# Scores on four 32-row tiles with a bank each, and the products with the values in two blocks per group

## The chip, the cores and the metric

One NeuronCore of a Trainium2 chip runs the whole kernel. The metric is the device time of one execution in microseconds, lower is better. Engines: TensorE (PE in the profile, PEld for its weight loads), VectorE (DVE), ScalarE (ACT), GpSimd (POOL), SyncE (SP).

## The reference

A Flamingo-like layer: gated cross attention with 16 heads of 16, then a gated mixture of 8 experts with the two best per token. B = 32 batches, S = 56 query rows, T = 1500 context rows, D = 256. Only the attention is touched:

```python
q = proj(layernorm(x), Wq, bq)              # (B, 16, 56, 16)
k = proj(ctx, Wk, bk)                       # (B, 16, 1500, 16)
v = proj(ctx, Wv, bv)
scores = einsum('bhsd,bhtd->bhst', q, k) / 4
scores = clip(where(attend, scores, -10000), -50, 50)
probs = softmax(scores)
ctx = einsum('bhst,bhtd->bhsd', probs, v)
delta = layernorm(clip(rs, 0, 0.3) * (ctx @ Wo.T + bo)) * gamma + beta
x = x + tanh(g_xattn) * delta
x = x + tanh(g_ffn) * experts(layernorm(x))
```

## The kernel before, in words

The work goes by pairs of batches, 16 pairs. A batch's 1500 context rows are three groups of 500 (GC = 4 chunks of TC = 125 rows each), so a pair has six groups, q = 0 to 5, and 24 chunks. A step u on ScalarE and VectorE is two chunks, half a group. Everything is unrolled, each engine has one list of instructions in a fixed order, and semaphores alone tie the lists together.

All fp32 products of keys, values and scores are made of three terms in fp32r, high by high, high by low, low by high. `kv_part` (L578) makes keys and values of the group after the current one. It has four calls per group: half 0 or 1 (which 128 key columns, which two value chunks), part 0 or 1 (which 64 rows of the contraction). Keys run on one 64-row half of the array and values on the other at the same time; k_ps has a bank for each half, v_ps is one bank.

`scores` (L613) makes one chunk: positions in the partitions, heads by queries in the columns. The head dimension is 16, so four heads (64 rows) are taken in one product: the keys of 125 positions are the weights, and q_hi / q_lo, where each head's queries stand in columns of their own with zeros elsewhere (`q_diagonal`, L1110, with hmask), stream as 4 x 56 = 224 columns. Two such 64-row tiles run at a time, r = 0 and 1, each into its own bank; the two column blocks m share the bank. Chunks of even and odd number use two banks each out of the four of sc_ps, so that `scores` of one chunk can run while ScalarE reads the other (`wait(pe, exp_done, n - 1)`, L621).

`exps` (L892) is ScalarE's exponential of one chunk into prob, `clip` (L1273) VectorE's clamp, and `pv` (L631) the product of the probabilities with the values: 16 heads on four 32-column tiles with plain fp32, summed over a batch in o_ps. The keys leave k_ps in two steps: `k_hi_evac` (L878, the instruction is L883) on ScalarE and then `k_lo_evac` (L1057, L1060) on VectorE, which needs the first. `v_evac_step` (L1069, L1075) on VectorE empties v_ps.

TensorE's order in a group (`pair`, L711) is: PV of the four chunks of the group before, side work of `beside_pv`, part (0,0) of the next group's keys and values, scores of chunk c, part (0,1), scores of c + 1 and c + 2, part (1,0), scores of c + 3, part (1,1). Side work is there at q = 3 (ranks and router, query projection, output projection) and q = 5 (two transposes). Its results share a bank with the keys' second half, so it waits for `k_lo`. The first scores of a group wait for that group's low keys (L620).

Of the kernel before, what the change touches and what calls it, by code (L numbers as in the profile page):

```python
# [31 lines left out]
HW = HS * HD  # L32
NE = 8
# [21 lines left out]
CST = (P, NE, HS, KD, KD, PW, NE, NE * NE, CAP // SL, NU, 1, 2 * NS)  # L55
# [9 lines left out]
def gated_cross_attention_moe(nc, a, slot_rows, expert_rows, sums_dram, inv_dram, out):  # L65
# [5 lines left out]
    with ExitStack() as ctx:  # L71
# [121 lines left out]
        q_hi = sb("q_hi", [P, 2, KD, HS, S], fp32r, scope=att)  # L193
        q_lo = sb("q_lo", [P, 2, KD, HS, S], fp32r, scope=att)
# [346 lines left out]
        def _(pe):  # L541
# [71 lines left out]
            def scores(i, c):  # L613

                n = i * PC + c
                b, g = c // NC, c // GC
                if c % NC == 0:
                    pe.wait_ge(q_ready, 4 * i + 2 * b + 2)
                if c % GC == 0:
                    pe.wait_ge(k_lo, KD * (i * PG + g + 1))  # L620
                wait(pe, exp_done, n - 1)  # L621
                cs = slice(c % GC * TC, (c % GC + 1) * TC)
                for m in range(KD):
                    for term, (k, q) in enumerate(((kh, q_hi), (kh, q_lo), (kl, q_hi))):
                        for r in range(2):
                            rows = slice(r * HW, (r + 1) * HW)
                            last = pe.matmul(sc_ps[0:TC, 2 * (c % 2) + r, m * HS * S:(m + 1) * HS * S],  # L627
                                             k[rows, g % 2, m, cs], q[rows, b, m, :, :], start=term == 0, stop=term == 2)
                last.then_inc(scores_done, 1)

            def pv(i, c):  # L631
# [7 lines left out]
                for h in range(NH):  # L639
                    col, q = divmod(h, ST)  # L640
                    at = (h // HS % 2 * KD + h // (2 * HS)) * HS + h % HS
# [69 lines left out]
            def pair(i):  # L711
# [13 lines left out]
                for q in range(PG):  # L725
# [3 lines left out]
                    if first and q == 1:  # L729
                        pe.wait_ge(o_clear, 1)  # L730
                    if not (first and q == 0):
                        for d in range(GC, 0, -1):
                            pv(*((i, c - d) if q > 0 else (i - 1, PC - d)))
                    beside_pv(i, q, first, late, final)
                    if more:
                        kv_part(n, 0, slot, 0)
                    scores(i, c)
                    if more:
                        kv_part(n, 0, slot, 1)
                    if first and q == 0:  # L740
                        pe.wait_ge(v_evac, 2)
                    scores(i, c + 1)
                    if not more:
                        turn(0)
                    scores(i, c + 2)
                    if more:
                        kv_part(n, 1, slot, 0, freed.get(q, ()))
                    scores(i, c + 3)
                    if more:
                        kv_part(n, 1, slot, 1)  # L750
                    if q == PG - 2:
                        whole_lines(i)
# [124 lines left out]
        def _(act):  # L877
# [14 lines left out]
            def exps(i, c):  # L892

                n = i * PC + c
                act.wait_ge(scores_done, n + 1)
                wait(act, pv_done, n - PB + 1)
                act.activation(prob[0:TC, c % PB, :].rearrange("p (c n) -> p c n", c=2),  # L897
                               sc_ps[0:TC, 2 * (c % 2):2 * (c % 2) + 2, 0:NH * S // 2], ACT.Exp,
# [41 lines left out]
            def pair(i, first=False, late=False, final=False):  # L940
                for u in range(UN):
# [20 lines left out]
                    if half == 1:  # L962
                        exps(i, 2 * u + 1)
                    if not (final and q == PG - 1):
                        k_hi_evac(i * PG + q + 1, half, (q + 1) % 2)
                    if half == 0:
                        exps(i, 2 * u + 1)
# [64 lines left out]
        def _(dve):  # L1032
# [77 lines left out]
            def q_diagonal(dst, b, part):  # L1110
                shape = [P, KD, HS, S]
# [167 lines left out]
            def pair(i, first=False, late=False, final=False):  # L1279
                for u in range(UN):  # L1280
# [5 lines left out]
                    if u == 10 and not first:  # L1286
                        y_low(i - 1)
                    if half == 0:
                        if more:
                            v_evac_step(i * PG + q + 1, half, (q + 1) % 2)  # L1290
                        clip(i, 2 * u)
# [277 lines left out]
```

## Time and profile before

| | us |
|---|---|
| median of 3 runs | 1195.04 |
| lowest, highest | 1194.09, 1195.85 |
| profiled execution | 1202.38 |
| its span, first to last instruction | 1200.3 |
| TensorE's mean granted clock over the span, share of full | 0.981 |
| busy: TensorE products, loads | 1130.6, 1082.1 |
| busy: VectorE, ScalarE, GpSimd | 862.1, 664.2, 156.8 |

Products on TensorE are pipelined: a product's duration includes its way through the array, so the pace is read from the distance of starts, not from the durations. The attention stage fills the time up to about 1080 us, the experts the rest.

### The profile page before, as it was taken

How to read it: one execution, taken by the hardware profiler on the slowest of the kernel's cores; microseconds unless marked ns; L12 is line 12 of the kernel's file. 1: busy time of each engine (PE TensorE's matmuls, PEld its weight loads, DVE VectorE, ACT ScalarE, POOL GpSimd, SP SyncE). 2: the span in 40 equal slices, each digit the busy share in tenths (PEclk: the TensorE clock that was granted, in tenths of full speed). 3: DMA queues.
4: the chain of work that ended last, by engine and by line, in shares of the span. 5: the costliest groups of instructions: out<-in, count | busy, mean ns of one | idle time of the engine just before them, and what ended most of it. 6: DMA issues, size and time to landing. Idle time of an engine off the chain costs nothing.

```text
span 1200.3 us, 56000 instructions
## 1 busy us (share of the span) xinstructions
PE 1130.6 (94%) x24824; PEld 1082.1 (90%) x24824; DVE 862.1 (72%) x2003; ACT 664.2 (55%) x846; POOL 156.8 (13%) x186
## 2 busy tenths in 40 slices
PE   4799999999999999999999999999999999969884
PEld 4799999999999999999999999999999999968874
DVE  4467776777777776777777777777777777757677
ACT  1466565655556565656565556656565656534432
POOL 0000100010010101010111101010101101023431
PEclk9799999999999999999999999999999999989998
DMA  4223132222323233323222232323321222124306
GB/s 153 74 74 91 57 93 79 85 76 77 91 88 91 67 87 93 80 63 94 83 86 68 89 91 88 87 71 87 93 78 50 79 61 71 30 54 120 90 25 169
DMA packets 59487, 98.57 MB, mean 82 GB/s; under 512 B 14514, under 2 KB 42034, under 8 KB 59250
## 3 DMA queue, kind: packets, MB, share of 16 engines
q1 hardware_dynamic: 49538, 79.55, 23.9%
q10 hardware_dynamic: 6832, 8.92, 2.1%
q0 software_dynamic: 2880, 6.53, 1.5%
q8 instruction: 199, 3.26, 1.1%
q14 instruction: 38, 0.31, 0.1%
HBM read 70.32 MB, written 24.71 MB: 79 GB/s over the span
## 4 chain that ended last, share of the span: by engine, by line
PE 86%; issue 5%; DVE 5%; DMA 2%; POOL 1%; ACT 1%; SPq 0%; DVEq 0%; POOLq 0%; ACTq 0%
PE v_ps L601 22%; PE k_ps L604 21%; PE sc_ps L627 20%; PE o_ps L642 13%; PE k_ps L659 1%; PE sc_ps L544 1%; PE sc_ps L545 1%; PE k_ps L666 1%; PE sc_ps L546 1%; PE v_ps L692 1%; DVE acc L1509 1%; DVE h_sq L1438 1%; DVE acc L1452 1%; POOL rstd L460 0%; PE k_ps L805 0%
## 5 line engine op out<-in xcount | busy, mean ns | idle before, releaser
L897 ACT ACTIVATE prob<-sc_ps,m_bias 125x896 f32<-125x896 f32 x384 | 377.9, 1009 | 329.7 <-PE sc_ps L627 329.3
L601 PE MATMUL v_ps<-wv_hi,c_hi 64*125 64x256 f32 x1520 | 312.0, 285 | 2.7 <-DVE c_lo L1066 2.6
L604 PE MATMUL k_ps<-c_hi,wk_hi 64*128 64x500 f32 x760 | 306.8, 404 | 0.0
L601 PE MATMUL v_ps<-wv_lo,c_hi 64*125 64x256 f32 x1520 | 302.1, 279 | 0.0
L601 PE MATMUL v_ps<-wv_hi,c_lo 64*125 64x256 f32 x1520 | 301.9, 278 | 0.0
L604 PE MATMUL k_ps<-c_lo,wk_hi 64*128 64x500 f32 x760 | 294.0, 387 | 0.0
L604 PE MATMUL k_ps<-c_hi,wk_lo 64*128 64x500 f32 x760 | 293.2, 386 | 0.0
L1075 DVE TENSOR_TENSOR vst<-v_ps,rowv 125x512 f32<-125x512 f32 x191 | 131.3, 687 | 184.9 <-PE v_ps L601 184.9
L1277 DVE TENSOR_SCALAR prob<-prob 125x896 f32<-125x896 f32 x384 | 235.5, 626 | 21.3 <-ACT prob L897 21.1
L601 PEld LDWEIGHTS v_ps<-wv_hi,c_hi 64*125 64x125 f32 x1520 | 227.0, 185 | 16.6 <-issue 5.7
L627 PE MATMUL sc_ps<-q_hi,kh 64*125 64x224 f32 x1536 | 231.1, 268 | 7.1 <-ACT prob L897 7.1
L627 PE MATMUL sc_ps<-q_hi,kl 64*125 64x224 f32 x1536 | 232.5, 270 | 0.6 <-issue 0.6
L627 PE MATMUL sc_ps<-q_lo,kh 64*125 64x224 f32 x1536 | 232.7, 271 | 0.0
L601 PEld LDWEIGHTS v_ps<-wv_hi,c_lo 64*125 64x125 f32 x1520 | 230.4, 184 | 0.0
L601 PEld LDWEIGHTS v_ps<-wv_lo,c_hi 64*125 64x125 f32 x1520 | 229.3, 183 | 0.0
L627 PEld LDWEIGHTS sc_ps<-q_hi,kh 64*125 64x125 f32 x1536 | 198.7, 186 | 7.8 <-ACT prob L897 7.3
L642 PE MATMUL o_ps<-prob,vst 125*17 125x56 f32 x12288 | 179.9, 214 | 13.1 <-issue 8.5
L642 PEld LDWEIGHTS o_ps<-prob,vst 125*17 125x17 f32 x12288 | 158.7, 98 | 33.9 <-issue 25.6
L627 PEld LDWEIGHTS sc_ps<-q_hi,kl 64*125 64x125 f32 x1536 | 169.9, 187 | 1.0 <-issue 0.7
L627 PEld LDWEIGHTS sc_ps<-q_lo,kh 64*125 64x125 f32 x1536 | 168.4, 186 | 0.0
L883 ACT ACTIVATE kh<-k_ps,cst 128x500 fp32r<-128x500 f32 x192 | 130.3, 679 | 66.7 <-PE k_ps L604 66.7
L604 PEld LDWEIGHTS k_ps<-c_lo,wk_hi 64*128 64x128 f32 x760 | 142.3, 187 | 0.0
(193 smaller groups left out, 1664.3 us busy)
## 6 DMA issues: line engine op xcount, KB each, us to landing
raw<-in_ctxT SPq DMA_DIRECT2D x96, 500.0 KB, 3.8
slot_rows<-zero_row SPq DMA_DIRECT2D x112, 132.0 KB, 3.7
rows<-slot_rows SPq DMA_DIRECT2D x32, 132.0 KB, 2.1
w_raw<-in_we ACTq DMA_DIRECT2D x16, 256.0 KB, 5.1
rec<-inv_scratch SPq DMA_DIRECT2D x64, 56.0 KB
expert_out<-expert_rows SPq DMA_DIRECT2D x6, 448.0 KB, 7.3
xq<-in_x ACTq DMA_DIRECT2D x16, 112.0 KB, 4.0
xr<-in_x ACTq DMA_DIRECT2D x16, 112.0 KB, 3.7
```

The costliest lines, as they stand in the source:

```text
L544: pe.matmul(ps, w_h, m_h, start=first, stop=False)
L545: pe.matmul(ps, w_h, m_l, start=False, stop=False)
L546: return pe.matmul(ps, w_l, m_h, start=False, stop=last)
L601: v_last = pe.matmul(v_ps[0:TC, j * D:(j + 1) * D], c_s[v_rows, cs], w_m[v_rows, k, :], start=begin and j == 0, stop=end, skip_group_check ...
L604: k_last = pe.matmul(k_ps[:, half, 0:TG], w[k_rows, k, ws], c_m[k_rows, :], start=begin, stop=end)
L627: last = pe.matmul(sc_ps[0:TC, 2 * (c % 2) + r, m * HS * S:(m + 1) * HS * S], k[rows, g % 2, m, cs], q[rows, b, m, :, :], start=term == 0, ...
L642: last = pe.matmul(o_ps[q * 32:q * 32 + VW, col * S:(col + 1) * S], vst[0:TC, c // GC % 2, c % GC, h, :], prob[0:TC, c % PB, at * S:(at + ...
L659: last = pe.matmul(bank[:, m * PW:(m + 1) * PW], wq[:, k, m * P:(m + 1) * P], xnT[:, k, :], start=(k == 0), stop=(k == KD - 1))
L883: act.activation(kh[:, s, m, :], k_ps[:, m, 0:TG], ACT.Identity, bias=bk[:, m:m + 1]).then_inc(k_hi, 1)
L897: act.activation(prob[0:TC, c % PB, :].rearrange("p (c n) -> p c n", c=2), sc_ps[0:TC, 2 * (c % 2):2 * (c % 2) + 2, 0:NH * S // 2], ACT.Ex ...
L1075: dve.tensor_tensor(vst[0:TC, s, 2 * half:2 * half + 2, :, 0:HD], v_bank[0:TC, :].rearrange("p (j h d) -> p j h d", j=2, h=NH), bv[0:TC, : ...
L1277: dve.tensor_scalar(p, p, EXP_LO, EXP_HI, ALU.max, ALU.min).then_inc(clip_done, 1)
```

## The change

A product of the scores takes two heads, 32 rows, and 2 x 56 = 112 columns. Four tiles of 32 rows run side by side, each into a bank of its own. Two chunks are made in one call, and a bank holds both chunks' two column blocks; so a call of `scores` waits for all exponentials before it. Products and loads per chunk double from 12 to 24. `exps` reads one half of each of the four banks, 896 elements as before. In `pair` the order is: side work, scores of c and c + 1, parts (0,0) and (0,1), scores of c + 2 and c + 3, PV of c and c + 1, part (1,0), part (1,1), PV of c + 2 and c + 3. ScalarE takes both exponentials of a step ahead of the high keys. VectorE empties the value bank between the two clips in the first half, and after them in the second.

```diff
+QH = 2
+QW = QH * HD
-        q_hi = sb("q_hi", [P, 2, KD, HS, S], fp32r, scope=att)
-        q_lo = sb("q_lo", [P, 2, KD, HS, S], fp32r, scope=att)
+        q_hi = sb("q_hi", [P, 2, KD, QH, S], fp32r, scope=att)
+        q_lo = sb("q_lo", [P, 2, KD, QH, S], fp32r, scope=att)
...
-            def scores(i, c):
+            def scores(i, c0):
...
-                wait(pe, exp_done, n - 1)
-                cs = slice(c % GC * TC, (c % GC + 1) * TC)
-                for m in range(KD):
-                    for term, (k, q) in enumerate(((kh, q_hi), (kh, q_lo), (kl, q_hi))):
-                        for r in range(2):
-                            rows = slice(r * HW, (r + 1) * HW)
-                            last = pe.matmul(sc_ps[0:TC, 2 * (c % 2) + r, m * HS * S:(m + 1) * HS * S],
-                                             k[rows, g % 2, m, cs], q[rows, b, m, :, :], start=term == 0, stop=term == 2)
-                last.then_inc(scores_done, 1)
+                wait(pe, exp_done, n)
+                for c in (c0, c0 + 1):
+                    cs = slice(c % GC * TC, (c % GC + 1) * TC)
+                    for m in range(KD):
+                        at = (c % 2 * KD + m) * QH * S
+                        for term, (k, q) in enumerate(((kh, q_hi), (kh, q_lo), (kl, q_hi))):
+                            for r in range(ST):
+                                rows = slice(r * QW, (r + 1) * QW)
+                                last = pe.matmul(sc_ps[0:TC, r, at:at + QH * S], k[rows, g % 2, m, cs], q[rows, b, m, :, :],
+                                                 start=term == 0, stop=term == 2, tile_position=(r * QW, 0))
+                last.then_inc(scores_done, 2)
...
-                    at = (h // HS % 2 * KD + h // (2 * HS)) * HS + h % HS
+                    at = (h % (NH // KD) // QH * KD + h // (NH // KD)) * QH + h % QH
...
-                    if first and q == 1:
-                        pe.wait_ge(o_clear, 1)
-                    if not (first and q == 0):
-                        for d in range(GC, 0, -1):
-                            pv(*((i, c - d) if q > 0 else (i - 1, PC - d)))
                     beside_pv(i, q, first, late, final)
+                    if first and q == 0:
+                        pe.wait_ge(v_evac, 2)
+                    scores(i, c)
                     if more:
                         kv_part(n, 0, slot, 0)
-                    scores(i, c)
-                    if more:
                         kv_part(n, 0, slot, 1)
-                    if first and q == 0:
-                        pe.wait_ge(v_evac, 2)
-                    scores(i, c + 1)
-                    if not more:
+                    else:
                         turn(0)
                     scores(i, c + 2)
                     if more:
+                        if first and q == 0:
+                            pe.wait_ge(o_clear, 1)
+                        for d in range(2):
+                            pv(i, c + d)
                         kv_part(n, 1, slot, 0, freed.get(q, ()))
-                    scores(i, c + 3)
-                    if more:
                         kv_part(n, 1, slot, 1)
+                        for d in range(2, GC):
+                            pv(i, c + d)
...
-                act.wait_ge(scores_done, n + 1)
+                act.wait_ge(scores_done, n + 2 - c % 2)
                 wait(act, pv_done, n - PB + 1)
-                act.activation(prob[0:TC, c % PB, :].rearrange("p (c n) -> p c n", c=2),
-                               sc_ps[0:TC, 2 * (c % 2):2 * (c % 2) + 2, 0:NH * S // 2], ACT.Exp,
+                at = c % 2 * KD * QH * S
+                act.activation(prob[0:TC, c % PB, :].rearrange("p (r n) -> p r n", r=ST),
+                               sc_ps[0:TC, :, at:at + KD * QH * S], ACT.Exp,
...
                     exps(i, 2 * u)
-                    if half == 1:
-                        exps(i, 2 * u + 1)
+                    exps(i, 2 * u + 1)
                     if not (final and q == PG - 1):
                         k_hi_evac(i * PG + q + 1, half, (q + 1) % 2)
-                    if half == 0:
-                        exps(i, 2 * u + 1)
...
+                    clip(i, 2 * u)
+                    if half == 1:
+                        clip(i, 2 * u + 1)
+                    if more:
+                        v_evac_step(i * PG + q + 1, half, (q + 1) % 2)
                     if half == 0:
-                        if more:
-                            v_evac_step(i * PG + q + 1, half, (q + 1) % 2)
-                        clip(i, 2 * u)
-                        if more:
-                            k_lo_evac(i * PG + q + 1, half, (q + 1) % 2)
                         clip(i, 2 * u + 1)
-                    else:
-                        clip(i, 2 * u)
-                        clip(i, 2 * u + 1)
-                        if more:
-                            v_evac_step(i * PG + q + 1, half, (q + 1) % 2)
-                            k_lo_evac(i * PG + q + 1, half, (q + 1) % 2)
+                    if more:
+                        k_lo_evac(i * PG + q + 1, half, (q + 1) % 2)
```

## Rows read from the trace of the kernel before

**Rows 1.** The page: busy time of the engines, and the chain that ended last by line.

```profile
PE 1130.6 (94%) x24824; PEld 1082.1 (90%) x24824; DVE 862.1 (72%) x2003; ACT 664.2 (55%) x846; POOL 156.8 (13%) x186
...
PE v_ps L601 22%; PE k_ps L604 21%; PE sc_ps L627 20%; PE o_ps L642 13%; PE k_ps L659 1%; PE sc_ps L544 1%; PE sc_ps L545 1%; PE k_ps L666 1%; PE sc_ps L546 1%; PE v_ps L692 1%; DVE acc L1509 1%; DVE h_sq L1438 1%; DVE acc L1452 1%; POOL rstd L460 0%; PE k_ps L805 0%
```

**Rows 2.** Table by stretch: busy time (instructions) per engine, clock, DMA.

```profile
611.80:621.88 10.08, 10.08 (x252) 9.83 (x252) 7.23 (x14) 6.20 (x7) 0.00 (x0) 1.00 0.25 69
...
600.00:665.20 65.20, 64.45 (x1515) 61.77 (x1514) 48.60 (x112) 38.45 (x45) 7.80 (x9) 1.00 0.28 83
```

**Rows 3.** Chain in order of time, one group: start us, us, what.

```profile
611.80 1.30 PE sc_ps L627 x20
...
616.54 1.72 PE o_ps L642 x128
...
621.88 1.30 PE sc_ps L627 x19
```

**Rows 4.** Timeline of TensorE's products: start us, us, engine, line, out<-in, shape.

```profile
599.83 0.27 PE L627 MATMUL sc_ps<-q_hi,kh 64*125 64x224 f32 x2
...
601.03 0.28 PE L627 MATMUL sc_ps<-q_hi,kl 64*125 64x224 f32 x2
```

**Rows 5.** Timeline of TensorE's weight loads, the same scores.

```profile
599.84 0.19 PEld L627 LDWEIGHTS sc_ps<-q_lo,kh 64*125 64x125 f32 x2
```

**Rows 6.** Timeline of weight loads, router and query projection.

```profile
583.62 0.18 PEld L678 LDWEIGHTS k_ps<-wr,yT_hi 128*112 128x112 f32 x1
...
583.91 0.18 PEld L681 LDWEIGHTS k_ps<-wr,yT_hi 128*112 128x112 f32 x1
584.01 0.97 PEld L659 LDWEIGHTS k_ps<-xnT,wq 128*128 128x128 f32 x8
584.90 0.71 PEld L666 LDWEIGHTS k_ps<-wo,rec 128*112 128x112 f32 x4
```

**Rows 7.** Timeline of weight loads, last experts (224 columns stream).

```profile
1159.92 0.19 PEld L545 LDWEIGHTS sc_ps<-yT_lo,we_hi 128*128 128x128 f32 x1
...
1160.70 0.19 PEld L546 LDWEIGHTS sc_ps<-yT_hi,we_lo 128*128 128x128 f32 x1
```

**Rows 8.** Timeline, around one PV block of an ordinary group.

```profile
626.35 0.28 PE L601 MATMUL v_ps<-wv_hi,c_lo 64*125 64x256 f32 x1
...
626.56 1.77 PE L642 MATMUL o_ps<-prob,vst 125*17 125x56 f32 x128
626.66 0.68 ACT L883 ACTIVATE kh<-k_ps,cst 128x500 fp32r<-128x500 f32 x1 [0.35 <-PE k_ps L604]
...
628.30 0.35 PE L601 MATMUL v_ps<-wv_hi,c_hi 64*125 64x256 f32 x1
```

**Rows 9.** Timeline, head of a group with side work, q = 3.

```profile
581.91 0.68 ACT L883 ACTIVATE kh<-k_ps,cst 128x500 fp32r<-128x500 f32 x1 [0.35 <-PE k_ps L604]
...
582.74 0.73 DVE L1060 SCALAR_TENSOR_TENSOR kl<-k_ps,cst,kh 128x500 fp32r<-128x500 f32 x1
583.52 0.21 PE L703 MATMUL k_ps<-cum_b,ones 112*112 112x8 bf16 x1
...
585.96 0.38 PE L601 MATMUL v_ps<-wv_hi,c_hi 64*125 64x256 f32 x1
```

**Rows 10.** Chain in order of time, head of the group q = 5.

```profile
604.73 1.02 PE o_ps L642 x72
...
607.64 0.34 PE k_ps L651 x2
...
608.17 0.32 PE v_ps L601
```

**Rows 11.** Groups by line: count | busy us, mean ns | idle before, releaser.

```profile
L897 ACT ACTIVATE prob<-sc_ps,m_bias 125x896 f32<-125x896 f32 x384 | 377.9, 1009 | 329.7 <-PE sc_ps L627 329.3
...
L1277 DVE TENSOR_SCALAR prob<-prob 125x896 f32<-125x896 f32 x384 | 235.5, 626 | 21.3 <-ACT prob L897 21.1
...
L1075 DVE TENSOR_TENSOR vst<-v_ps,rowv 125x512 f32<-125x512 f32 x191 | 131.3, 687 | 184.9 <-PE v_ps L601 184.9
```

## What I expect of the change, and why

> **What bounds the kernel now.** I read the page first: its busy shares and its chain of waits. TensorE is busy for 1130.6 of 1200.3 us, and the chain that ended last lies mostly on it, by line 22% products for the values (L601), 21% for the keys (L604), 20% scores (L627) and 13% products with the values, PV (L642) [rows 1]. So in the attention stage TensorE's own order of work is the path. Next I read the table by stretch. One ordinary group of 500 context positions takes 10.08 us, a pair of batches with its six groups 65.20 us, both with TensorE full and its clock at the full level, 2.4 GHz [rows 2]. The chain in order of time gives the period again: the two middle score chunks start at 611.80 and at 621.88, one PV block stands between them and takes 1.72 us for four chunks, two chunks of scores take 1.30 [rows 3]. The rest is the key and value parts: with 1.74 from the start of PV to the next part [rows 8] and 2.61 for four chunks of scores, 10.08 - 1.74 - 2.61 = 5.73, that is 1.43 for each of four parts with its entry and exit.
>
> The question is what a pair of score products costs. Two products on the two row halves start together, and the pairs follow one another at (601.03 - 599.83)/11 = 0.109 us [rows 4]. A product streams 224 columns, 0.093 us at 2.4 GHz. Its weight load has 125 columns and starts with the product before it [rows 5]. Which of the two sets 0.109? Three other places answer. The router's loads of 112 columns, with only 8 or 16 columns to stream, follow at (583.91 - 583.62)/3 = 0.097; the query projection's loads of 128 columns with 112 to stream at (584.90 - 584.01)/8 = 0.111 [rows 6]; the last experts' loads of 128 columns with 224 to stream at (1160.70 - 1159.92)/7 = 0.111 [rows 7]. So 112 or 224 streamed columns make no difference, and the pace follows the loaded columns: 112, 125, 128 give 0.097, 0.109, 0.111, each some 4 ns over columns/1.2 GHz. The scores are paced by their weight loads.
>
> **The change part by part.**
>
> **Scores on four tiles.** A chunk still has two column blocks and three terms, so each row tile still loads 6 x 125 columns; only the streamed columns halve, from 224 to 112. By rows 4 to 7 a slot stays at 0.109 and a chunk at 0.65 us: nothing gained. There are now 24 load and product pairs in a chunk. PV shows that TensorE can take them: 128 pairs in 1.72 us, 13.4 ns a pair [rows 3], where the new scores need 27 ns. That four tiles load at once is not in the trace, which shows two (rows 5) and, in PV, four column tiles; bounds below. ScalarE reads the same 896 elements of a chunk, 1.01 us [rows 11].
>
> **Switches of the array's division.** Today keys, values and scores all use 64-row tiles, and only PV differs. Into PV, the step from the last value product is 0.21 us [rows 8], where two value products follow at about 0.11 to 0.12, so 0.10 more. Out of PV: the next part starts 1.74 after the block's start, some 0.03 more than its pairs take, and its first product lasts 0.35 where one in the middle lasts 0.28 [rows 8]: 0.10 in all. After the change a group has scores, parts, scores, PV, parts, PV: six switches instead of two. Those between 32-row and 64-row tiles are not in the trace; bounds are 0 (as between keys and scores now, both 64 rows) and, with a margin of as much again for a row division never seen, 0.20. I take 0.10, nearer to PV, since the row division changes too. The Trainium skill's page "TensorEngine Tiling (Array Packing)", Key Properties, says that changing the tiling mode drains the engine; no run here shows it for row tiles of two sizes, and by it the upper bound would hold.
>
> **The body of a group**, from the first score product s0 to T, the end of the second pair of key and value parts: scores 1.31, switch 0.10, parts 2.80, switch 0.10, scores 1.31, switch 0.10, PV of two chunks 0.85, switch 0.10, parts up to the end of their last product 2.96. Sum 9.63. Before, the body from the first part to T is 10.08 less the stretch from T to the next part. ScalarE's read of the keys starts 0.03 after T, at 626.66, so T = 626.63, and the next part starts at 628.30 [rows 8]: 1.67, and a body of 8.41. The new body is 1.22 longer: half of PV has moved into it, and the switches.
>
> **The head of a group**, from T to the next first product. Now PV of four chunks and half of the next key and value products lie between the last key product and the scores that need its keys. After the change only two chunks of PV do, 0.85 us. What must end is: ScalarE writes the high part of the keys, VectorE empties the value bank (0.69 [rows 11], beside it), VectorE writes the low part. One traced case: key part ended 581.88, ScalarE from 581.91, low part from 582.74 for 0.73, TensorE's next product 583.52, 50 ns after that [rows 9]. There VectorE came from clips; with clips out of the way the low part starts when the high part is done, 0.03 + 0.68 + 0.05 = 0.76 after T, and ends at 1.49. Then 0.05 and 0.10 for the first product: 1.64. So PV covers some 0.9 of it and TensorE stands for about half a microsecond in every group, a wait that is not there now. Behind the waiting scores everything on TensorE is queued. An ordinary group: 1.64 - 1.67 + 1.22 = +1.19 us, 11.27 us in all.
>
> **The two groups with side work.** Before the products of q = 3 TensorE already waits for the low keys, since the side results share their bank. Side work runs from 583.52 to 585.96, 2.44 us [rows 9]. Head before 585.96 - 581.88 = 4.08; after 1.54 + 2.44 = 3.98; with the body +1.12. At q = 5 the head now has gaps in PV: PV starts at 604.73 (T is the same within 0.02) and the parts at 608.17, 3.40 to 3.44 us, of which the side work is 608.17 - 607.64 = 0.53 [rows 10]. After, 1.54 + 0.53 = 2.07, which gives 2.07 - 3.40 + 1.22 = -0.11, if the gaps don't return elsewhere.
>
> **Other steps, taken at nothing.** The scores' four banks are no longer double buffered: the next two chunks wait for both exponentials, 2.02 us plus 0.2 after the scores' end. The parts between, 2.8 us and two switches, cover that with 0.7 to spare; without cover it would be 2.2 us a time. The clips (0.63 each [rows 11]) now stand behind the value bank in the first half; PV of chunk c+1 needs the clip some 1.4 us after the parts' end, and scores of 1.31, a switch and the first chunk's PV (0.43) come first. In the groups with routing work VectorE's clips may end 0.2 us after T, which I leave to the range. The query spreads halve on VectorE, off the path. First and last groups: no change of note.
>
> **Sum.** A pair: 4 x 1.19 + 1.12 - 0.11 = 5.77. There are 96 groups, so 95 heads: 95/6 x 5.77 = 91 us. Against the profiled execution's own 1202.38 us that is 1294; it stands 7.3 us over the median of the runs, 1195.04, so **1287 us**. Its own range: no cost of switches between 64 and 32 rows takes off 0.2 x 95 = 19; twice the price for all five that aren't hidden adds 0.5 x 95 = 48; so 1268 to 1335.
>
> **The rivals.**
>
> **Streaming sets the pace, not the loads (faster).** If a 32-row tile's load were hidden or shorter, a slot would fall to 112 columns, 0.047 + 0.004, or to four pairs at PV's 13.3 ns, 0.053. Then a chunk takes 0.32, a group saves 4 x 0.33 = 1.32 us and 96 groups 127 us: 1287 - 127 = **1160 us**. It wins from the point where a group saves more than the 0.96 us that switches and head add on average, a slot under 0.069. For it: no row shows a load into a 32-row tile. Against it: rows 6 and 7, where streaming 8 or 112 or 224 columns left the pace to the loads. The Trainium skill's page "TensorE: Matmul & The Clock Gate", Part 3, tells of four row tiles whose products start some 4 ns apart, 3.07 times as fast; the products there stream 512 columns, and by it this rival would hold. The same page, LDWEIGHTS, has the load go by columns and not by rows, which speaks for my forecast; with it the trace agrees (112 columns and 128 columns, rows 6).
>
> **Loads of four tiles share two paths (much slower).** A slot becomes 2 x 0.109, a chunk 1.31, +2.6 us a group: 1287 + 250 = 1537. Against it: PV keeps four loads going at 13.3 ns each, below the 17/1.2 = 14.2 ns that one load of 17 columns would stream; but those are column tiles.
>
> **Switches are free.** Then 4 x 0.10 go from the body, 38 us: 1249. It stays slower, by the wait at the head and PV's lost overlap with it.
>
> **How the numbers follow.** Forecast 0.66, within 1268 to 1335. Free switches or a shorter head, 1215 to 1268: 0.10. Streaming at full gain, about 1160: 0.14. Partly shorter slots, 1165 to 1215: 0.03. Over 1335, by partly shared loads, fetches or full sharing: 0.07, of it 0.04 up to 1350. From 1215 to 1350 that is 0.80. Faster by over 0.2% (2.4 us, about what a measurement of this kernel can tell from no change): 0.16. Within it: 0.02. Slower: 0.82.
>
> **What the profile after would show.** Score products with 112 columns in fours, the fours 0.109 apart: right; 0.05 to 0.07: the first rival; 0.2: the second. A chain step through the high keys (L883) and low keys (L1060) into the scores in each group, TensorE idle for about 0.5 us before the scores with VectorE's keys as the releaser: right. Steps of 0.2 us between the last score product and the first key product: the switches. Ordinary groups of 11.27 us. The prediction fails if the fours come faster than 0.07, or if the head is hidden in some way that I don't see.

## The result, and the profile after

| | before | after |
|---|---|---|
| median of 4 runs, us | 1194.57 | 1437.56 |
| lowest, highest | 1193.16, 1195.85 | 1430.90, 1446.44 |
| profiled execution, span | 1202.38, 1200.3 | 1433.35, 1431.3 |
| mean granted clock over the span | 0.981 | 0.964 |

The changed kernel takes 1.204 times as long (95% interval 1.196 to 1.212), 243 us more. Slower was forecast, but only by 92 us, and 1437.56 lies well above the range that ended at 1350.

The page after: busy time, granted clock in 40 slices, one line on TensorE's instruction queue, and the chain that ended last by engine and by line (to be read against rows 1).

```profile
PE 1268.9 (89%) x29432; PEld 1149.1 (80%) x29432; DVE 881.9 (62%) x2003; ACT 653.5 (46%) x846; POOL 152.6 (11%) x186
...
PEclk8899999999999999999999999999999999998998
...
q8 instruction: 235, 3.85, 1.1%
...
PE 77%; DVE 11%; issue 8%; DMA 2%; POOL 1%; ACT 1%; SPq 0%; ACTq 0%; DVEq 0%; POOLq 0%
PE v_ps L603 24%; PE sc_ps L631 19%; PE k_ps L606 18%; PE o_ps L646 7%; DVE kl L1059 4%; DVE vst L1074 4%; PE sc_ps L546 1%; PE k_ps L663 1%; PE sc_ps L547 1%; PE sc_ps L548 1%; PE k_ps L670 1%; PE v_ps L696 1%; DVE acc L1504 1%; DMA wq<-in_wq 0%; PE k_ps L655 0%
```

TensorE's share falls from 94% to 89%, and VectorE's keys and value bank stand in the chain with 8%, where they had no share worth a name. The instruction queue moves 3.85 MB in 235 packets, that is 16 KB each; the page before shows 199 packets and 3.26 MB on this queue. TensorE has 2 x (29432 - 24824) = 9216 instructions more, products and loads, and the 36 packets more on this queue make 256 of them each.

One ordinary group, in the timeline of TensorE's products with ScalarE's and VectorE's steps at the head (start us, duration us, engine, line, out<-in, shape, count):

```profile
702.32 0.98 PE L646 MATMUL o_ps<-prob,vst 125*17 125x56 f32 x64
702.39 0.68 ACT L884 ACTIVATE kh<-k_ps,cst 128x500 fp32r<-128x500 f32 x1 [2.37 <-PE k_ps L606]
702.43 0.69 DVE L1074 TENSOR_TENSOR vst<-v_ps,rowv 125x512 f32<-125x512 f32 x1 [0.62 <-PE v_ps L603]
...
703.11 0.74 DVE L1059 SCALAR_TENSOR_TENSOR kl<-k_ps,cst,kh 128x500 fp32r<-128x500 f32 x1
...
703.90 0.32 PE L631 MATMUL sc_ps<-q_hi,kh 32*125 32x112 f32 x4 [0.60 <-DVE kl L1059]
704.05 0.28 PE L631 MATMUL sc_ps<-q_lo,kh 32*125 32x112 f32 x4
704.16 0.28 PE L631 MATMUL sc_ps<-q_hi,kl 32*125 32x112 f32 x4
...
705.15 0.28 PE L631 MATMUL sc_ps<-q_hi,kl 32*125 32x112 f32 x4
...
705.35 0.38 PE L603 MATMUL v_ps<-wv_hi,c_hi 64*125 64x256 f32 x1
...
706.64 0.40 PE L603 MATMUL v_ps<-wv_hi,c_lo 64*125 64x256 f32 x2
...
707.18 0.35 PE L603 MATMUL v_ps<-wv_hi,c_hi 64*125 64x256 f32 x1
...
708.76 0.32 PE L631 MATMUL sc_ps<-q_hi,kh 32*125 32x112 f32 x4
```

Three things are to be seen. The score products come in fours, 0.11 us apart, at the pace of the pairs in rows 4, though each streams half the columns. At the head, PV is done after 0.98 us and TensorE stands idle for 0.60 until the low keys are written. And between the two adjacent key and value parts there is a hole: the last two value products start from 706.64 on, and the next part starts only at 707.18, although nothing but products for keys and values stands there. That hole wasn't in the forecast. The table of waits of the weight loads names it (us in total, times, longest):

```profile
PEld v_ps L603 <- PE k_ps L606: 63.7, 190, 0.6
PEld sc_ps L631 <- DVE kl L1059: 35.1, 46, 0.8
PEld sc_ps L631 <- issue: 32.5, 47, 1.7
```

190 times, twice a group, the load for the second part waits for the last key product of the first. The third line is a wait without a releaser, up to 1.7 us. From score to score, an undisturbed group of the changed kernel takes 12.21 us (1150.68 to 1162.89 in the chain), where 11.27 was forecast and 10.08 stands in rows 2. A pair takes 77.0 to 85.6 us, on average 79.7 (14 pairs between GpSimd's first steps for the experts' weights, 125.65 to 1241.31), where 71.0 was forecast.

### The profile page after: what moved, and what is told of

It reads as the page before. It is cut to its first block, busy times and chain, and to the rows that moved or that the text cites. A ratio compares the mean times of both kernels' runs of the same rounds, so it can differ in the third digit from the quotient of the medians.

```text
span 1431.3 us, 65217 instructions
## 1 busy us (share of the span) xinstructions
PE 1268.9 (89%) x29432; PEld 1149.1 (80%) x29432; DVE 881.9 (62%) x2003; ACT 653.5 (46%) x846; POOL 152.6 (11%) x186
## 3 DMA queue, kind: packets, MB, share of 16 engines
q8 instruction: 235, 3.85, 1.1%
## 4 chain that ended last, share of the span: by engine, by line
PE 77%; DVE 11%; issue 8%; DMA 2%; POOL 1%; ACT 1%; SPq 0%; ACTq 0%; DVEq 0%; POOLq 0%
PE v_ps L603 24%; PE sc_ps L631 19%; PE k_ps L606 18%; PE o_ps L646 7%; DVE kl L1059 4%; DVE vst L1074 4%; PE sc_ps L546 1%; PE k_ps L663 1%; PE sc_ps L547 1%; PE sc_ps L548 1%; PE k_ps L670 1%; PE v_ps L696 1%; DVE acc L1504 1%; DMA wq<-in_wq 0%; PE k_ps L655 0%
## 5 line engine op out<-in xcount | busy, mean ns | idle before, releaser
L603 PE MATMUL v_ps<-wv_hi,c_hi 64*125 64x256 f32 x1520 | 343.4, 306 | 31.6 <-DVE c_lo L1065 3.0
L606 PE MATMUL k_ps<-c_hi,wk_hi 64*128 64x500 f32 x760 | 342.9, 451 | 0.4 <-issue 0.3
L631 PE MATMUL sc_ps<-q_hi,kh 32*125 32x112 f32 x3072 | 228.7, 282 | 51.6 <-DVE kl L1059 28.6
L631 PE MATMUL sc_ps<-q_lo,kh 32*125 32x112 f32 x3072 | 221.0, 271 | 6.8 <-issue 6.8
L631 PE MATMUL sc_ps<-q_hi,kl 32*125 32x112 f32 x3072 | 221.0, 271 | 1.7 <-issue 1.7
L631 PEld LDWEIGHTS sc_ps<-q_hi,kh 32*125 32x125 f32 x3072 | 155.4, 186 | 82.9 <-DVE kl L1059 35.1
L646 PE MATMUL o_ps<-prob,vst 125*17 125x56 f32 x12288 | 193.1, 215 | 5.7 <-DVE prob L1276 5.1
L631 PEld LDWEIGHTS sc_ps<-q_lo,kh 32*125 32x125 f32 x3072 | 157.4, 187 | 7.0 <-issue 6.9
L631 PEld LDWEIGHTS sc_ps<-q_hi,kl 32*125 32x125 f32 x3072 | 157.9, 188 | 2.6 <-issue 2.5
L606 PEld LDWEIGHTS k_ps<-c_hi,wk_lo 64*128 64x128 f32 x760 | 146.1, 192 | 0.0
```

Of the source, the lines that this page charges most:

```text
L603: v_last = pe.matmul(v_ps[0:TC, j * D:(j + 1) * D], c_s[v_rows, cs], w_m[v_rows, k, :], start=begin and j == 0, stop=end, skip_group_check ...
L606: k_last = pe.matmul(k_ps[:, half, 0:TG], w[k_rows, k, ws], c_m[k_rows, :], start=begin, stop=end)
L631: last = pe.matmul(sc_ps[0:TC, r, at:at + QH * S], k[rows, g % 2, m, cs], q[rows, b, m, :, :], start=term == 0, stop=term == 2, tile_posit ...
L646: last = pe.matmul(o_ps[q * 32:q * 32 + VW, col * S:(col + 1) * S], vst[0:TC, c // GC % 2, c % GC, h, :], prob[0:TC, c % PB, at * S:(at + ...
```

## Experiments

Each ratio is to the kernel before on the same chip. The chips differ by 0.8% in that kernel: 1194.99 us for the first four runs told here as one set (fewer columns, the order without the tiles, PV in one block on four tiles, whole packets), 1203.94 for the next four, 1202.48 for the last four. Between sets I therefore compare ratios, and give their difference times 1195 us.

### Streaming fewer columns

```diff
+                            heads = HS if term == 0 else HS // 2
-                            last = pe.matmul(sc_ps[0:TC, 2 * (c % 2) + r, m * HS * S:(m + 1) * HS * S],
-                                             k[rows, g % 2, m, cs], q[rows, b, m, :, :], start=term == 0, stop=term == 2)
+                            last = pe.matmul(sc_ps[0:TC, 2 * (c % 2) + r, m * HS * S:(m * HS + heads) * S],
+                                             k[rows, g % 2, m, cs], q[rows, b, m, 0:heads, :], start=term == 0, stop=term == 2)
```

> The kernel before, but in the second and third term of every score product only two of the four heads stream, 112 columns in place of 224 (the other two heads lose their low-order terms). Loads, their number and everything else are as before. If the weight loads set the pace (0.109 us for 125 columns): no change, 1194 us within 3. If streaming set it: two thirds of the 2304 slots fall from 0.109 to about 0.056, 81 us less, about 1114.

Measured: 1195.3 us, ratio to before 1.0006 (0.9995 to 1.0017). A third fewer columns stream in the scores, and the time stays. So on 64-row tiles it isn't the stream that sets their pace. On 32-row tiles the trace after shows the same distance, 0.109 us for four products of 112 columns, each with its load of 125. Both fit loads that set the pace, and the first rival, at 1160 us, falls.

### The order without the tiles

The changed kernel with the scores, the spread queries and the exponential's addresses of the kernel before:

```diff
-                            for r in range(ST):
-                                rows = slice(r * QW, (r + 1) * QW)
-                                last = pe.matmul(sc_ps[0:TC, r, at:at + QH * S], k[rows, g % 2, m, cs], q[rows, b, m, :, :],
-                                                 start=term == 0, stop=term == 2, tile_position=(r * QW, 0))
+                            for r in range(2):
+                                rows = slice(r * HW, (r + 1) * HW)
+                                last = pe.matmul(sc_ps[0:TC, 2 * (c % 2) + r, m * HS * S:(m + 1) * HS * S],
+                                                 k[rows, g % 2, m, cs], q[rows, b, m, :, :], start=term == 0, stop=term == 2)
```

> The changed kernel's order on all engines, but the scores on two 64-row tiles again (224 columns, two banks per chunk, 12 products per chunk). Theory: the order of the work costs, not the four tiles. The scores keep their 0.65 us per chunk, two switches of 0.10 us per group go (19 us), and TensorE's list is 9216 instructions shorter, so some of the gaps in the middle of the scores and the half-clock stretches behind them go: 1385 to 1420 us. Rival, four tiles are what costs: back near 1290 or below.

Measured: 1358.39 us, ratio 1.137 (1.135 to 1.139), below the 1385 to 1420 expected. So the order of the work costs 163 us and the four tiles 79 (1437.56 - 1358.39). The clock stays full in the whole of 100 to 1000 us, and an ordinary group takes 11.95 us (710.10 to 722.05) in its chain in order of time:

```profile
710.10 1.57 PE sc_ps L630 x24
...
713.11 0.14 issue
713.24 0.35 PE v_ps L603
...
718.74 0.14 issue
718.88 0.35 PE v_ps L603
720.55 0.02 issue
720.58 0.69 DVE vst L1072
721.27 0.73 DVE kl L1057
722.00 0.04 issue
722.05 1.57 PE sc_ps L630 x24
```

The 0.14 of "issue" ahead of a value product of 0.35 marks the hole between two parts, twice a group. At the head the chain leaves TensorE and runs through the value bank and the low keys. Undisturbed groups differ by 12.21 - 11.95 = 0.26 us because of the four tiles, 25 us in 95 groups. The other 54 us are not in undisturbed groups; the next runs look for them.

### PV in one block, on 32-row and on 64-row tiles

```diff
-                        if first and q == 0:
-                            pe.wait_ge(o_clear, 1)
-                        for d in range(2):
-                            pv(i, c + d)
                         kv_part(n, 1, slot, 0, freed.get(q, ()))
                         kv_part(n, 1, slot, 1)
-                        for d in range(2, GC):
+                        if first and q == 0:
+                            pe.wait_ge(o_clear, 1)
+                        for d in range(GC):
                             pv(i, c + d)
```

With four tiles:

> The changed kernel, but PV of all four chunks stands in one block behind the last key part, ahead of the next group's scores. Theory: the wait for the low keys at the head (0.6 us idle per group) is covered by 1.7 us of PV, and two switches go; a group falls by about 0.66 us, 63 us in all, and fewer long idle stretches leave the clock high: 1360 to 1380. If the head isn't a cost of its own: 1437 less 19 for the switches, 1418.

Measured: 1474.39 us (1457.02 to 1479.68), ratio 1.229 (1.221 to 1.237): slower than the changed kernel, against the forecast. The profiled execution is the longest of the four, 1479.68 us. The wait at the head is gone, and an undisturbed group takes 11.42 us (711.37 to 722.79), as expected. But the table of waits has other long lines (us in total, times, longest), and the next group of the chain in order of time shows a hole in the middle of the scores:

```profile
PE o_ps L646 <- issue: 42.5, 30, 2.6
PE sc_ps L631 <- issue: 29.7, 24, 2.9
```

```profile
722.79 0.68 PE sc_ps L631 x16
723.47 1.09 issue
724.56 1.08 PE sc_ps L631 x31
```

With 64-row tiles:

> The changed kernel's order with the scores on two 64-row tiles (the run with 1358 us), but PV of four chunks in one block ahead of the next group's scores. With 32-row tiles this block removed the wait at the head (group 12.2 to 11.4 us undisturbed) and yet cost time, by long gaps without any releaser and half clock. Theory: those gaps come from TensorE's list, which was denser there; with 64-row tiles the gain stays: 11.95 - 0.75 = 11.2 us a group, 1280 to 1300 us. Rival, the PV block itself brings the gaps: above 1358.

Measured: 1295.43 us, ratio 1.076 (1.075 to 1.078), within what was expected. The same edit gains 72 us (1.137 to 1.076) on 64-row tiles, with 56 001 instructions in the kernel, and loses 30 us (1.204 to 1.229) on 32-row tiles, with 65 217. So the wait at the head was real, and with four tiles something eats the gain. A pair takes 71.0 us here (396.61 to 467.58). The chain in order of time of an ordinary group:

```profile
716.21 1.70 PE o_ps L645 x128
...
720.85 0.14 issue
720.98 0.35 PE v_ps L603
...
727.13 0.71 PE o_ps L645 x47
```

This group takes 10.92 us, and no other engine stands in it. It has one PV block, 64-row tiles and two switches, as the group of 10.08 us in the kernel before. What differs on TensorE is that its parts stand together in two places. So a place where a part follows a part costs (10.92 - 10.08)/2 = 0.42 us.

### Whole packets of instructions

```diff
+                    for _ in range(32):
+                        pe.sem_inc(pe_filler, 1)
                     scores(i, c)
```

> The changed kernel with 32 more semaphore increments ahead of each group's first scores on TensorE's list, 192 per pair, which makes a pair's list longer by a quarter of 16 KB times three, so that its length is again a whole number of 16 KB packets (before: 12 by estimate, changed: 14.25, this: 15). Theory: the irregular gaps of 0.6 to 1.7 us are TensorE waiting for its instructions; they then come at the same place in each pair, the time moves by up to 30 us either way, and the runs differ less from each other. Rival, the gaps come from something else: they stay irregular.

Measured: 2056.76 us. The run didn't test what it was made for. The increments aren't cheap: a gap of 4.1 to 4.8 us stands ahead of the scores of each group, some 0.14 us for each of 32, and the mean granted clock falls to 0.792. The chain in order of time:

```profile
701.21 4.10 issue
705.30 2.77 PE sc_ps L631 x41
```

A whole undisturbed block of 48 products takes 1.45 us in the changed kernel. The 41 products right behind the gap take nearly twice that, at half clock: this is what a gap can cost beyond itself.

The kernel before has 5 or 10 such increments per pair. Without them:

```diff
-FILL = 10
+FILL = 0
```

> The kernel before without the 10 (or 5) semaphore increments at the end of q = 4 of each pair. 32 of them cost some 4.4 us in the run with whole lines, 0.14 each; the kernel before shows two gaps of together 0.7 us per pair at that place. Theory: they cost 5 x 0.14 us in 13 pairs and 10 x 0.14 in three, and half of it is hidden behind the wait for the low keys: 5 to 12 us faster, 1183 to 1190. Rival, the increments hold TensorE's list in step with its 16 KB packets and save gaps elsewhere: 1195 or slower, with irregular gaps.

Measured: 1209.53 against 1203.94 us, ratio 1.0039 (1.0025 to 1.0053). Slower by 6 us where 5 to 12 less was expected, so the rival holds: the increments pay for themselves. Without them PV's waits without a releaser last up to 2.1 us (0.5 in the kernel before), in total 14.9 us against 8.5, and one half-clock stretch appears in the attention stage. Of the gaps without a releaser of 0.15 us or more 12, with 6.7 us in all, end 1.2 to 1.6 us after an instruction packet; in the kernel before there are 2, with 0.6 us. So it seems to matter to this kernel where TensorE's packets of instructions begin, though the run also takes time out of the list. The changed kernel's pair is longer by 576 instructions, 2.25 packets of 256, so that the places wander.

### Less data on the DMA engines

These two kernels leave out three quarters of the context's columns from the third group on; the engines' work keeps its shapes.

```diff
-                sp.dma_start(raw[:, s, :, :], a["ctxT"][bass.ds(n, 1)].squeeze(0)).then_inc(raw_in[s], 16)
+                sp.dma_start(raw[:, s, :, 0:TC], a["ctxT"][bass.ds(n, 1)].squeeze(0)[:, :, 0:TC]).then_inc(raw_in[s], 16)
```

In the changed kernel:

> The changed kernel, but from the third group on only a quarter of the context's columns is loaded, the rest keeps the values of an earlier group. Theory: the gaps of 1 to 1.7 us without a releaser are TensorE's instruction packets held up behind data packets, and the half-clock stretches follow from them; with 36 MB less data most go: 1437 falls to 1385 to 1415 us and the mean clock from 0.96 to 0.98. Rival, the gaps don't depend on the transfers: 1430 to 1440 us.

Measured: 1402.9 us (1396.15 to 1407.16), ratio 1.165 (1.161 to 1.168) against 1.204 of the changed kernel, 47 us less. The two profiled executions, 1433.35 and 1407.16 us, are 26 us apart. In the order with PV in one block on four tiles:

> The same quarter load in the order with PV in one block on four 32-row tiles (the run with 1474 us, the one with the most gaps, an undisturbed group of 11.4 us). Theory as above: 1474 falls to 1340 to 1400 us. Rival, the gaps are the price of the dense list alone, whatever the transfers: 1460 to 1480 us.

Measured: 1388.66 us (1388.16 to 1389.86), ratio 1.155 (1.153 to 1.156) against 1.229, 89 us less. Of the two orders the one with more gaps gains more from fewer transfers, and with them the PV block is a gain, of 14 us (1388.66 against 1402.9), not yet of the 63 us once expected. Its waits without a releaser fall by half:

```profile
PE o_ps L646 <- issue: 21.1, 35, 1.4
PE sc_ps L631 <- issue: 14.9, 20, 1.8
```

The table by stretch of the changed kernel shows one such gap and what follows (us, busy time and instructions of PE, PEld, DVE, ACT, POOL, granted clock, DMA share, GB/s):

```profile
300.00:310.00 10.00, 9.35 (x204) 8.73 (x205) 4.17 (x8) 4.35 (x5) 1.42 (x2) 0.83 0.08 23
297.00:298.80 1.80, 1.19 (x68) 1.02 (x69) 1.77 (x3) 1.60 (x2) 0.00 (x0) 1.00 0.68 260
298.80:300.50 1.70, 0.02 (x4) 0.00 (x0) 1.43 (x6) 0.00 (x0) 0.70 (x1) 1.00 0.03 5
```

Four score products start at 298.50 after a wait of 0.61 for the low keys; then TensorE does nothing from 298.80 to 300.50. In the 1.8 us ahead of that the DMA engines are busy for 68%, and one instruction packet is among what they move: it runs from 298.17 to 299.13, and TensorE goes on 1.37 us after its end. In the next 10 us the clock is at 0.83 on average, which is a third of the stretch at 1.2 GHz, 1.7 us of clock missing. In all, 13 of the 98 stretches of 10 us from 60 to 1040 us have less than full clock, with 22 us of clock missing; in the run with the PV block on four tiles 41 of 98, with 65 us; in the kernel before and in the order without the tiles none. With the quarter load it is 12 of 98 and 17 us in the changed kernel, 13 and 19 us with the PV block.

### Parts kept apart, with and without the tiles

TensorE's order becomes part (0,0), scores, part (0,1), PV, part (1,0), scores, part (1,1), PV; `o_evac_step` moves one step later. The new order of calls, cut at the marks:

```python
                     if more:
                         kv_part(n, 0, slot, 0)
                     scores(i, c)
                     if more:
                         kv_part(n, 0, slot, 1)
...
                         for d in (2, 1):
                             pv(*((i, c - d) if q > 0 else (i - 1, PC - d)))
                     if more:
                         kv_part(n, 1, slot, 0, freed.get(q, ()))
                     scores(i, c + 2)
                     if more:
                         kv_part(n, 1, slot, 1)
...
                         for d in range(2):
                             pv(i, c + d)
```

> Four 32-row tiles as in the changed kernel, other order on TensorE: part (0,0), scores of c and c + 1, part (0,1), PV of the two chunks before c, part (1,0), scores of c + 2 and c + 3, part (1,1), PV of c and c + 1. No two parts follow one another, and PV and a part stand between the last keys and the scores that need them; the emptying of o_ps on VectorE moves one step later. Theory (measured so far: two waits between adjacent parts of about 0.5 us, a head idle for 0.6 us per group): both go, eight switches of 0.10 us stay, a group takes 10.6 to 10.8 us in place of 12.2; undisturbed 1275 to 1300 us, plus up to 60 us if gaps in TensorE's instructions and half-clock stretches come as in the changed kernel. Rival, four tiles cost by themselves: above 1340.

> The same order as the run before it, with the scores on two 64-row tiles and the list as short as in the kernel before. Theory: only PV switches the array, four times a group in place of two: 10.08 + 0.2 to 0.3 us a group, 1210 to 1230 us, no half-clock stretches in the attention stage. If emptying a bank, exponentials for two chunks in a row or the wait on all exponentials cost too: 1250 or more.

Measured: 1413.71 us on 32-row tiles (1.177, 1.173 to 1.181) and 1363.73 on 64-row tiles (1.133, 1.131 to 1.135), both far above what was expected. The order had brought a wait of its own. In the table of waits of the second, between 100 and 1000 us (us in total, times, longest):

```profile
PE v_ps L603 <- DVE vst L1075: 54.2, 73, 1.1
```

VectorE empties the value bank only after a clip that waits for an exponential, and part (1,0) waits for the bank. The mend, on top of the same order:

```diff
                     exps(i, 2 * u)
-                    exps(i, 2 * u + 1)
                     if not (final and q == PG - 1):
                         k_hi_evac(i * PG + q + 1, half, (q + 1) % 2)
+                    exps(i, 2 * u + 1)
...
+                    if more:
+                        v_evac_step(i * PG + q + 1, half, (q + 1) % 2)
                     clip(i, 2 * u)
-                    if half == 1:
-                        clip(i, 2 * u + 1)
                     if more:
-                        v_evac_step(i * PG + q + 1, half, (q + 1) % 2)
-                    if half == 0:
-                        clip(i, 2 * u + 1)
-                    if more:
                         k_lo_evac(i * PG + q + 1, half, (q + 1) % 2)
+                    clip(i, 2 * u + 1)
```

> The split order with 64-row tiles (the run with 1364 us), but VectorE empties the value bank before the clips in both halves and ScalarE writes the high keys between the two exponentials. There TensorE waited 1.1 us for the value bank before part (1,0), behind a clip that waited for an exponential. Theory: with that wait gone and no adjacent parts, 10.3 to 10.5 us a group, 1215 to 1240 us. If the order costs in another way: above 1280.

> The same, with four 32-row tiles: it differs from the run before it by the tiles alone. Theory: the scores themselves cost nothing more (0.109 us per four products), the four switches between 64-row and 32-row tiles 0.10 to 0.13 us each, 0.4 to 0.5 us a group, 40 to 50 us in all, plus 10 to 40 us for gaps in the denser list: 50 to 90 us over the run before it. If the tiles were free: within 10 us of it.

Measured: 1273.27 us (1.059, 1.057 to 1.061) and 1353.7 us (1.125, 1.123 to 1.127). An ordinary group of the first takes 10.50 us (601.50 to 612.00, as expected); its time is over the 1240 of the expectation because the groups with side work still wait, up to 1.5 us, for the low keys on VectorE, and because of six of the 98 stretches of 10 us with less than full clock. The two differ by the tiles alone: 80 us. The chain in order of time of the second shows the ordinary group at 11.19 us, 0.69 more than without the tiles, 66 us in 95 groups:

```profile
700.93 1.45 PE sc_ps L631 x48
...
712.12 1.45 PE sc_ps L631 x47
```

Four switches between 64-row and 32-row tiles stand in that group, so each costs about 0.17 us there; with PV in one block three more than without the tiles cost 11.42 - 10.92 = 0.50, 0.17 each; in the changed kernel's order two more cost 0.26, 0.13 each. Of the other 14 us, 12 are clock: between 60 and 1040 us 20.4 us of it are missing against 8.5.

This run has as long a list as the changed kernel, 65 218 instructions, and yet hardly a gap ahead of the scores' loads. Table of waits between 100 and 1000 us, first of this run, then of the changed kernel:

```profile
PEld sc_ps L631 <- issue: 1.4, 6, 0.2
...
PEld sc_ps L631 <- issue: 25.3, 35, 1.7
```

## Why the prediction was wrong

**The direction and the two reasons given for it hold.** The scores' slot stayed at 0.109 us (forecast 0.109), and the run with fewer streamed columns shows why. The wait for the low keys at the head came as forecast: 1.54 us from the end of the keys to the next scores (702.36 to 703.90), against the 1.64 forecast, with TensorE idle for 0.60. Exponentials for two chunks in a row were covered, as forecast. The side work's head ran as forecast too: the changed kernel's trace shows TensorE waiting for VectorE's low keys ahead of L655 and L707, 1.4 and 0.8 us at the longest.

**The step that failed is the body of a group.** I put a pair of adjacent parts at 2.80 and gave the parts in the new order the durations that they had in the old. But `kv_part` begins its second part with a wait for the end of the first (kpart_done and vpart_done, L588 and L589 before the change), since keys and values change halves of the array there and go on adding into the same bank. In the old order scores or PV always stood between the two, and the wait cost nothing; the change takes that cover away, and I had listed covers for the exponentials, the clips and the bank, but not for this wait. In the trace after, two parts and their exit take 708.76 - 705.35 = 3.41 us in place of 2.90, twice a group: 1.0 us a group. With it an undisturbed group would have been put at 12.27; it measured 12.21. Of this 1.0 the wait is 0.84, 80 us in 95 groups, by the run with 64-row tiles and PV in one block, which differs from the kernel before in TensorE's ordinary group by the two adjacent places alone (10.92 against 10.08). The rest goes with the switches around the parts. Keeping the parts apart agrees: it brought the 64-row group from 10.92 to 10.50 us, although it has two switches more.

**The second miss is in the rest over 1335, to which I gave 0.07 in all.** The shortest pair of the changed kernel takes 77.0 us, the mean is 79.7; times 15.8 pairs this is 42 us. It is made of gaps in which TensorE waits for nothing that the table of waits can name, mostly in the scores, and of stretches at half clock.

The trace has the time of every instruction packet, and it ties the gaps to them. In the attention stage of the changed kernel eight gaps without a releaser last over 1 us (1.02 to 1.68). In all eight TensorE goes on 1.31 to 1.50 us after the end of a packet. In the order with one PV block on four tiles 32 of 35 such gaps end 1.30 to 1.59 us after one; a moment picked at random has a packet's end 1.2 to 1.6 us behind it in 7% of cases. So these gaps are waits for instructions, as far as such an agreement can show it. The packets ahead of the eight gaps are no slower than others, 0.95 us against 1.05 on average, so they must have started late. What makes them late stays open in part. That the transfers have a share in it is shown: with the quarter load no gap of this kind over 1 us is left in the changed kernel, and it is 47 us faster, the order with the PV block 89. The length of the list alone doesn't bring the gaps: the last run with parts kept apart on four tiles is as long and has hardly any in its scores. In its order a part always stands between scores and PV, whose pairs of load and product follow at 27 and 13 ns, closer than anywhere else in the group. That it is such dense pieces side by side that outrun the packets is my reading, and not tested.

The lost clock isn't all due to these gaps. Of eleven stretches at 1.2 GHz between 60 and 1040 us seven begin at such a gap or within 2.3 us behind it, two behind waits of 1.28 us for the low keys, and two with neither close ahead. With the quarter load the gaps over 1 us are gone, and 17 of the 22 us of missing clock are still there.

**The switches** between 32-row and 64-row tiles cost 0.13 to 0.17 us, not 0.10, within the bounds of 0 and 0.20. The Trainium skill's page "TensorEngine Tiling (Array Packing)", Key Properties, says that a change of tiling mode drains the engine. The runs on 64-row and 32-row tiles fit it, with a cost of 0.13 to 0.17 us a change; the drain itself stands in no trace.

**The sum again**, profiled execution against profiled execution, 231 us: the shortest pair is 77.0 - 65.2 = 11.8 us longer, 187 us over 15.8 pairs. Of these 91 were forecast, and of the other 96 the wait between parts makes 80; gaps and clock make 42. That leaves 2 for the ends.

**The rivals.** Streaming as the pace: refuted, by the first experiment on 64-row tiles and by the distance of the fours on 32-row tiles. Shared loads of four tiles: refuted, the fours come 0.109 apart and not 0.218. Free switches: refuted by the pair of runs that differ in the tiles alone.

No order that was tried beats the kernel before: the best takes 1.059 times as long. There TensorE is full in the ordinary groups, with the same work as before and two switches more.

## What to carry to other kernels

Before halving what a product streams, find out whether the stream or the weight load sets the pace: compare the distance of starts where streams differ and loads are alike. When work is moved out from between two pieces, list every wait that stood behind it, those of an engine on itself too, since a wait that costs nothing in the old order shows in no table. Look also for short gaps without a releaser on the bounding engine, and compare their ends with the times of the instruction packets: here they ended with them, and most of the gaps over 1 us had some microseconds at half clock behind them.

## What the runs showed of the hardware that I had not expected

- A score product's pace doesn't depend on the rows of its tile either: four tiles of 32 rows load 125 columns each and keep 0.109 us, as two of 64 rows do.
- One semaphore increment on TensorE's list costs some 0.14 us, where a pair of PV's load and product costs 13 ns.
- Each of the changed kernel's eight gaps of over 1 us without a releaser ended 1.31 to 1.50 us after the end of an instruction packet of 16 KB.
- A gap's length alone doesn't tell whether the clock falls. In the changed kernel seven of those eight gaps (1.02 to 1.68 us) had a stretch at 1.2 GHz at their end or soon behind it. In the 64-row order with the parts apart and VectorE early, only one of 20 waits of 1.05 to 1.38 us for the low keys had one. Gaps of 0.6 us, one in nearly every group of the run without the tiles, had none (granted clock 1.00 from 100 to 1000 us).
- With the same TensorE list, cutting the context's loads to a quarter made two orders 47 and 89 us faster, though past the first group (3.6 us) no wait for these loads stood in the changed kernel's chain.
